# A fused two-layer graph transformer on one core: the softmax division before each block transpose moves from GpSimd to VectorE

## The reference, cut to what matters

```python
nx = _ln(x, ln1_g, ln1_b)                      # x: (64, 128, 256)
q, k, v = nx @ wq + bq, nx @ wk + bk, nx @ wv + bv      # 8 heads of 32
bias = where(adj > 0, 0.1 * adj * adj, -inf)[:, None]
scores = einsum('bhqd,bhkd->bhqk', q, k) / sqrt(32) + bias
attn = softmax(scores, axis=-1)                # 128x128 for each of 8 heads
x1 = x + (einsum('bhqk,bhkd->bhqd', attn, v) @ wo + bo)
x2 = x1 + gelu(_ln(x1, ln2_g, ln2_b) @ w1 + b1) @ w2 + b2
# layer 1: one head over 256 features, then a layer norm of x2 + out @ Wo + bo
w = softmax(where(adj == 0, -inf, (x2 @ Wq) @ (x2 @ Wk).T / 16))
y = layer_norm(x2 + (w @ (x2 @ Wv)) @ Wo + bo)
```

## Time and profile before

| | |
|---|---|
| time, median of 3 runs | 894.96 us (894.94 to 897.37) |
| the profiled execution: its time, and its span | 897.54 us, 895.8 us |
| TensorE busy, share of the span | 859.9 us, 96% |
| VectorE | 681.3 us, 76% |
| ScalarE | 605.3 us, 68% |
| GpSimd | 503.5 us, 56% |
| transfers | 87.11 MB, mean 97 GB/s |

### The profile page before, as it was taken

How to read it: one execution, slowest core, us unless ns; L and a number is a source line. 1 busy time by engine, 2 the same in 40 slices (tenths; PEclk the granted TensorE clock), 3 DMA queues, 4 the chain that set the end, 5 groups by cost and what they waited for, 6 DMA issues and landing times.

```text
span 895.8 us, 22038 instructions
## 1 busy us (share of the span) xinstructions
PE 859.9 (96%) x7159; PEld 764.0 (85%) x7159; DVE 681.3 (76%) x2522; ACT 605.3 (68%) x1830; POOL 503.5 (56%) x374
## 2 busy tenths in 40 slices
PE   8899898799999999999999999999999999999896
PEld 8787687598898989889898988989898988989795
DVE  6685757878787887868788787878788787875736
ACT  5684854867857676776768676786866678584542
POOL 3522843647667474766657575666757476655312
PEclk9899999999999999999999999999999999999998
DMA  8000231533325242323415241431524233243001
GB/s 270 18 21 13 72 107 62 152 123 90 129 49 173 70 164 82 102 97 81 159 52 176 70 144 63 105 133 47 176 70 164 64 90 120 58 148 114 25 1 36
DMA packets 106304, 87.11 MB, mean 97 GB/s; under 512 B 3462, under 2 KB 91164, under 8 KB 106268
## 3 DMA queue, kind: packets, MB, share of 16 engines
q1 hardware_dynamic: 106252, 86.66, 31.6%
q10 hardware_dynamic: 16, 0.00, 0.0%
HBM read 47.85 MB, written 38.80 MB: 97 GB/s over the span
## 4 chain that ended last, share of the span: by engine, by line
PE 74%; DVE 5%; ACT 4%; issue 3%; POOL 3%; DMA 1%; SPq 0%; DVEq 0%; POOLq 0%; ACTq 0%
PE bank L401 20%; PE bank L403 19%; PE bank L402 19%; PE bank L562 3%; PE bank L687 3%; PE bank L586 3%; PE bank L718 3%; ACT p L1056 2%; DVE p L1458 1%; PE bank L668 1%; PE bank L497 1%; POOL p_s L1911 1%; DMA p_s<-parked 1%; DVE bank L1363 1%; DMA parked<-pT 1%
## 5 line engine op out<-in xcount | busy, mean ns | idle before, releaser
L992 ACT ACTIVATE p_s<-bank,neg_max 128x128 f32<-128x128 f32 x464 | 162.8, 393 | 78.8 <-DVE neg_max L1363 78.8
L1911 POOL TENSOR_TENSOR p_s<-p_s,rsum 128x512 f32<-128x512 f32 x116 | 118.2, 1040 | 91.3 <-DVE rsum L1370 70.9
L401 PE MATMUL bank<-w_hi,hT_hi 128*128 128x256 f32 x512 | 147.5, 288 | 1.2 <-DVE hT_lo L1255 1.2
L403 PE MATMUL bank<-w_hi,hT_lo 128*128 128x256 f32 x512 | 144.0, 281 | 0.0
L402 PE MATMUL bank<-w_lo,hT_hi 128*128 128x256 f32 x512 | 144.0, 281 | 0.0
L1363 DVE CUSTOM_DVE_ANT_0 bank<-bank,bias 128x128 f32<-128x128 f32 x464 | 117.3, 328 | 2.2 <-PE bank L562 2.2
L401 PE MATMUL bank<-n2T_hi,w_hi 128*128 128x512 f32 (+1 forms) x272 | 109.0, 401 | 5.3 <-DVE hT_lo L1255 5.2
L1023 ACT ACTIVATE bank<-bank,vec_cols 128x512 f32<-128x512 f32 (+1 forms) x136 | 86.6, 637 | 33.6 <-PE bank L403 28.0
L992 ACT ACTIVATION_READ_ACCUMULATOR p_s<-bank,neg_max 128x1 f32 x464 | 108.1, 233 | 0.0
L403 PE MATMUL bank<-n2T_hi,w_lo 128*128 128x512 f32 (+1 forms) x272 | 103.7, 381 | 0.0
L402 PE MATMUL bank<-n2T_lo,w_hi 128*128 128x512 f32 (+1 forms) x272 | 103.6, 381 | 0.0
(11 more groups left out here) (237 smaller groups left out, 2430.9 us busy)
## 6 DMA issues: line engine op xcount, KB each, us to landing
parked<-pT SPq DMA_DIRECT2D x116, 256.0 KB, 4.4
pT<-parked SPq DMA_DIRECT2D x15, 1024.0 KB, 5.6
p_s<-parked SPq DMA_DIRECT2D x14, 1024.0 KB, 7.7
xs<-in_x SPq DMA_DIRECT2D x15, 512.0 KB, 4.2
out<-y SPq DMA_DIRECT2D x14, 512.0 KB, 2.9
adj_i<-in_adj SPq DMA_DIRECT2D x15, 256.0 KB, 2.8
out<-y SPq DMA_DIRECT2D x3, 256.0 KB, 2.2
x2T_f<-in_L_gnn_w SPq DMA_DIRECT2D x1, 512.0 KB, 6.8
```

The source lines that it names most:

```text
L401: mm(out, a_hi, b_hi, start=first, stop=False)
L403: return mm(out, a_lo, b_hi, start=False, stop=last)
L992: last = run(to, of, ACT.Exp, scale=-1.0, bias=neg_max[:, r, place:place + 1], accum_out=psum[:, r, place:place + 1])
L1911: P.tensor_tensor(p_s[:, r, :, :], p_s[:, r, :, :], rsum[:, r, :, None].to_broadcast([128, 4, NODES]), ALU.mult).then_inc(pool_p, 1)
```

## The change

The multiplication by `rsum` is done by VectorE, as the first part of `blocks`: it waits for its own reciprocal, multiplies `p_s[:, r]` in place, waits for its own product, and transposes it. `normal` and its 116 instructions go from GpSimd, and with them the semaphore `pool_p`. All other instructions stay, in their order.

```diff
             def blocks(g, q, r):
-                dve.wait_ge(pool_p, blocks_done(g, q, r))
+                dve.wait_ge(dve_r, 4 * (pair0(g) + q) + r + 1)
+                V.tensor_tensor(p_s[:, r, :, :], p_s[:, r, :, :], rsum[:, r, :, None].to_broadcast([128, 4, NODES]),
+                                ALU.mult).then_inc(dve_p, 1)
+                dve.wait_ge(dve_p, 4 * (pair0(g) + q) + r + 1)
                 if r == 0:
...
-            def normal(g, q, r):
-                pool.wait_ge(dve_r, 4 * (pair0(g) + q) + r + 1)
-                P.tensor_tensor(p_s[:, r, :, :], p_s[:, r, :, :], rsum[:, r, :, None].to_broadcast([128, 4, NODES]),
-                                ALU.mult).then_inc(pool_p, 1)
...
             def turn(gp, ga, gb, gc):
...
                 offset(gc, size(gc))
-                for r in range(HPT):
-                    normal(gp, 0, r)
                 x2_plus_bo(gb)
-                if size(gp) > 2:
-                    for r in range(3):
-                        normal(gp, 1, r)
                 rstd(2, ga)
                 pool.wait_ge(ln_dve[2], ln_end(ga))
-                if size(gp) > 2:
-                    normal(gp, 1, 3)
                 x_plus_bo(gp)
```

More of the change, by code:

```diff
@@ L271, in build @@
         dve_s, dve_r, dve_p = sem("dve_s"), sem("dve_r"), sem("dve_p")
-        pool_p = sem("pool_p")
         dve_blocks = sem("dve_blocks")
@@ L1926, in first_turn @@
                 move_up(2)
-                for r in range(HPT):
-                    normal(2, 0, r)
             def second_turn():
@@ L1938, in second_turn @@
                 bias(3)
-                for r in range(HPT):
-                    normal(2, 1, r)
                 x2_plus_bo(1)
-                for r in range(HPT):
-                    normal(3, 0, r)
                 rstd(2, 2)
@@ L1949, in second_turn @@
                 move_up(3)
-                for r in range(HPT):
-                    normal(3, 1, r)
             def turn(gp, ga, gb, gc):
```

## The result

The changed kernel takes **946.36 us** (median of 4 runs, 944.09 to 946.66), the one before 894.95 (4 runs, 894.85 to 897.37): a ratio of **1.056**, with a 95% interval of 1.0542 to 1.0579, so 48.5 to 51.8 us more. The profiled execution took 944.09, the lowest of its runs, while that of before (897.54) lay above all of its own, so the two spans differ by 46.5 us only. Two single executions further down, 1670.53 us in e7 and 4171.74 in the kernel before beside it, were slow ones that no ratio counts; without the first, e7's median of 940.43 is 939.33.

What follows compares the result with a forecast made beforehand. TensorE bounds the looped turns, so only VectorE results reaching it late cost time: 1.7 + 0.2 + 0.4 + 1.1 = 3.4 us a turn, 40.8 over 12 turns, plus 9 in the start-up, together 50, giving 945 us; range 922 to 974.

Steps and rivals of the forecast that it cites:

- the start-up: Groups 2 and 3 before the looped turns: 16 blocks where TensorE already waits on VectorE; 9 us, between 3 and 14.
- group 16: Its four blocks: residual2 0.3 us late, but an out_project still stands ahead of x2_transpose on TensorE; costs nothing.
- The block: VectorE's product plus transpose for one bank: from 0.63 to 1.36 us, 0.73 more, 5.8 a turn for eight.
- First step, x2: First pair's blocks make VectorE's second residual2 late, so TensorE waits 1.7 us a turn at x2_transpose.
- Second step: After the second norm: TensorE waits 0.2 us for t_copy and 0.4 for biased1 at n2_transpose; sum so far 2.3.
- Third step, the holds: VectorE's last two products and GpSimd's adds block each other in SBUF until one ends; TensorE waits 1.1 us at mlp_up.
- The Trainium skill's rule: VectorE with two SBUF inputs contends with GpSimd reading SBUF, the later blocked throughout; without it the turn's sum stays 2.3.
- No holds (928): Rival: products and GpSimd's adds miss each other; 27.6 us in the turns, 5.6 in the start-up, 928; chance 0.17.
- GpSimd not letting go (971): Rival: GpSimd runs both adds without letting VectorE between; mlp_up waits 3.1 us, 5.4 a turn, 971; chance 0.12.
- The clock falling each turn (966): Rival: TensorE's clock drops after each turn's wait, 3.4 us at half speed, 1.7 more a turn, 966; chance 0.15.

Runs made afterwards that it cites:

- e7: Changed kernel with GpSimd's x_plus_bo moved ahead of its rstd of the second norm and x1_plus_b2 started only after VectorE's last product of the turn: 940.43 us, ratio 1.0496.
- e9: Changed kernel with VectorE's product cut from 128x512 to four elements a row, all other instructions kept: 897.56 us, ratio 1.0016.
- e2: Kernel before, with VectorE dividing only the first pair of each group and GpSimd the second as before: 921.38 us, ratio 1.0277.
- e4: Changed kernel with residual2 of the second pair moved ahead on VectorE, behind one part of biased instead of three: 942.37 us, ratio 1.0517.
- e8: e4 with residual1 straight behind residual2, and ScalarE's exponentials and VectorE's inverse of the second pair moved behind x2T's copies and low parts: 942.61 us, ratio 1.0521.
- e10: Changed kernel with GpSimd's x_plus_bo and x1_plus_b2 of every turn cut to 4 of 256 columns: 933.16 us, ratio 1.0409.
- e5: Changed kernel with VectorE's vo_copy moved ahead of the last two products and transposes of a turn: 955.66 us, ratio 1.0667.
- e3: Kernel before, with VectorE dividing only the second pair of each group and GpSimd the first as before: 922.41 us, ratio 1.0305.
- e1: Changed kernel with GpSimd's x_plus_bo and x1_plus_b2 in each looped turn started only after the turn's last transpose: 982.67 us, ratio 1.0971.
- e11: Changed kernel with VectorE's copies of t's second half and, in the turns, of vo given to ScalarE: 941.05 us, ratio 1.0497.
- e6: Changed kernel with GpSimd's x1_plus_b2 alone started only after VectorE's last product of the turn: 940.40 us, ratio 1.0491.

## Why the prediction was right

The time was forecast at 945 us, and 946.36 was measured. Its terms: 3.4 us a turn forecast, 3.29 measured; 9 in the start-up, 9.4 measured; nothing in group 16, nothing measured. They add up to 50 in the forecast and to 48.5 in the traces, so that the medians agree a little better than the sums; part of the 51.4 between them may be when the runs began.

- **The block.** 1.36 was forecast, 1.32 measured (477.02 to 478.37 is 1.35, 478.37 to 479.69 is 1.32). The product out of SBUF has the length of the one out of PSUM, 0.65 to 0.69, where nothing holds it. e9 shows that its length is the price: with it gone, all but about 1 us of the cost is gone.
- **First step, x2.** 1.7 forecast, 1.48 measured, mis-sized by the 0.04 a block and by what the first `residual2` found behind the first block: it came no later at all instead of 0.07. The second one was 1.86 late instead of 2.07. e2 has this step alone: 1.56 a turn. As a price it was right; that it is a place at which time could be won back was not (e4, e8).
- **Second step.** Sum 2.3 forecast, and 2.05 measured at `n2_transpose` (1.48 at x2, 1.87 at `scores1`). Its two terms came out the other way round: 0.39 instead of 0.2 for `t_copy`, 0.18 instead of 0.4 for `biased1`. `ve` fell to 0.17, as forecast. e10, the change without holds in the turns, costs 2.27 a turn: the forecast's 2.3.
- **Third step, the holds.** 1.2 to 1.6 us for the last two products was forecast, 1.30 and 1.53 measured, ended by the 0.55 after each hold that was worked out from the start-up. Their price was 1.1 and is 1.0 (e10). But the place was wrong. The prediction took them to end in a wait of 1.1 at `mlp_up`. It left out that `vo_copy`, between the two products, is waited for by the second half of `project_v`, which stands ahead of `mlp_up` on TensorE. From `n2_transpose` on, 0.78 us are lost there (2.83 less 2.05; a part of it is the wait of the first weight load for the same result), 0.25 at `mlp_up`, and 0.21 in the MLP's later blocks, for `hT_lo`. The sum was saved by both results lying on one nearly unbroken stretch of VectorE.
- **The Trainium skill's rule** (SBUF — State Buffer, "Who interferes with whom") that one engine blocks the other for a whole instruction is what e5 shows at its full size: 2.85 us for a product that comes 0.08 after GpSimd's add. The same section has a VectorE instruction with two SBUF inputs contend with any GpSimd instruction that reads SBUF; beside the mask below the product was not held (0.65).
- **The start-up.** The 9 us were a choice between 3 and 14 and not a sum, so that 9.4 came so near is luck in part. The waits of 2.46 and 2.11 grew to 6.32 and 4.46, two products of group 3 were held (1.63 and 2.12 us, at 153.92 and 156.22), and the granted clock was 0.61 for the 7 us behind the first wait. The prediction had nothing for the clock here. An estimate from these rows: 7 us at 0.61 lose 2.7, while before, 10.4 us behind the same wait at a mean of 0.84 lost 1.7, so about 1 of the 9.4 may be the clock's. How they split was not tried; e2 and e3 only show that either pair alone costs half.

**The rivals.** No holds (928): not so; e10, without them in the turns, is at 933.16. GpSimd not letting go (971): not so: in the twelve turns all 24 held products took 1.30 or 1.31 and 1.53 or 1.54, but e5 comes half way to it (955.66) by another road. The clock falling each turn (966): not so, it stayed at 1.00 with waits of 1.33 us, and of 1.55 in e5. In e1, whose turns hold a wait of 1.9 to 2.3 us and a second of 0.24 behind it in the turn shown above, it did fall: 0.63 over the 4 us from 526, between the levels of 1.2 and 2.4 GHz, in a kernel that took 982.67.

```profile
526.00:530.00 4.00, 3.39 (x8) 2.19 (x9) 3.36 (x8) 1.17 (x2) 1.97 (x3) 0.63 0.52 144
```

## What to carry to other kernels

An engine that is busy 76% of the span can, with some work added, become the bound of more than half a turn, though its idle time in all would hold the new work. Measure how long it runs there with next to no break, from the first instruction of the change to the last result for which the bounding engine waits, and price the change by that; which wait shows the loss is secondary, and reordering inside the stretch wins little. Where VectorE reads two tiles from SBUF while GpSimd works on SBUF, the product's price depends on its phase against GpSimd's instructions, from nothing to 2.2 us here, so each change of order nearby is a change of that price, and taking work away can be swallowed by it.

## What the runs showed of the hardware that was not expected

- VectorE was let in between two GpSimd adds that follow each other without a pause: each product held ended 0.55 us after the add under way (497.88 and 500.65 in the changed kernel, 505.79 in e5, 499.64 in e11). The next add is drawn from the end of the one before and lasts 2.82 or 2.83 us instead of 2.38 or 2.41 (497.28 in the changed kernel, 496.26 in e11). A product of four elements, held in the same way in e9, ended with the add.
- GpSimd's mask (`pen`, a scalar instruction with one input of 128x512) did not hold the product: in e5 the product of 506.47 lies inside the mask's 505.33 to 507.60 and took 0.65. In e10 one took 0.67 inside a mask too (494.47, in 492.84 to 495.02). The mask took 2.27 in e5 instead of the 1.94 or 1.95 of the kernel before and of e6. But it takes 2.27 in the changed kernel as well, where no product begins within it: in both a held product ends 0.46 us after the mask's start.
- A VectorE instruction of 128x4 with one input (`ve`) is held by a GpSimd add as by GpSimd's product before the change (0.66): 0.70 instead of 0.17 in e7, and 0.41 beside a copy in e6.
